# Five expert tiles instead of three started early, planned into the routing of the second batch

## What is computed

```python
x = _layernorm(x + _L0_attn_ref(...))     # causal attention, 16 heads of 16
x = _layernorm(x + _L0_ffn_ref(...))      # a linear map through an FFT, folded into one 256x256 matrix
x = _layernorm(x + _L1_attn_ref(...))     # attention over channels, one 256x256 matrix for each sequence
x = _layernorm(x + _L1_ffn_ref(...))      # 8 experts, one for each token
# the last block, on 4096 tokens:
aff = x @ centroids.T;  eid = argmax(aff);  alpha = sigmoid(sum(x * centroids[eid]))
xln = layernorm(x) * ln_g[eid] + ln_b[eid]
h = relu(xln @ w1[eid] + b1[eid])         # 256 -> 1024
out = x + alpha * (h @ w2[eid] + b2[eid]) # 1024 -> 256
```

## Time and profile before

| | us |
|---|---|
| median of 3 runs | 1402.43 (1398.66 to 1403.42) |
| the profiled execution, its own time | 1398.64 |
| its span, first to last instruction | 1396.9 |
| PE busy | 1334.6 (96%) |
| DVE busy | 1069.4 (77%) |
| ACT busy | 837.4 (60%) |
| POOL busy | 263.7 (19%) |

### The profile page before, as it was taken

The page is one execution under the profiler, slowest core; times in us unless marked ns, Lnnn a source line. Parts: engine busy times, 40 slices in busy tenths (PEclk is TensorE's granted clock), DMA queues, the critical chain, the costliest instruction groups (busy, mean ns, idle before and its releaser), DMA issues. The chain is left out here.

```text
span 1396.9 us, 45529 instructions
## 1 busy us (share of the span) xinstructions
PE 1334.6 (96%) x19106; PEld 805.1 (58%) x19106; DVE 1069.4 (77%) x1991; ACT 837.4 (60%) x1767; POOL 263.7 (19%) x440
## 2 busy tenths in 40 slices
PE   8999999999999999999999999899987799999998
PEld 3544334444444444444444444588765689999997
DVE  2567989989899899899898991566577666766766
ACT  3446668688788687787886886433455333333342
POOL 4332112102111121021021210100135411111111
PEclk9999999999999999999999999999999899999999
DMA  7796401212212212122310000314524665445441
GB/s 227 228 209 136 74 13 40 43 32 52 46 34 48 47 30 51 34 46 41 81 36 4 3 3 2 119 36 157 192 84 149 207 224 180 168 173 186 169 171 75
DMA packets 78230, 134.44 MB, mean 96 GB/s; under 512 B 12370, under 2 KB 64843, under 8 KB 72652
## 3 DMA queue, kind: packets, MB, share of 16 engines
q1 hardware_dynamic: 60556, 109.63, 26.9%
q10 hardware_dynamic: 14064, 13.47, 3.1%
q0 software_dynamic: 3408, 8.43, 1.8%
HBM read 68.01 MB, written 23.11 MB: 65 GB/s over the span
## 5 line engine op out<-in xcount | busy, mean ns | idle before, releaser
L1964 DVE TENSOR_REDUCE part_max<-pair 128x2 f32<-128x1024 f32 (+2 forms) x576 | 641.9, 1158 | 63.9 <-PE pair L1329 32.5
L1748 ACT ACTIVATE big<-pair 128x512 f32<-128x512 f32 (+1 forms) x1120 | 580.2, 607 | 151.6 <-PE pair L1360 143.5
L1360 PE MATMUL pair<-big 128*32 128x512 bf16 (+3 forms) x5120 | 347.5, 350 | 6.1 <-DMA big<-max_t 2.4
L1329 PE MATMUL pair<-big 128*32 128x512 bf16 (+3 forms) x5120 | 342.6, 349 | 9.3 <-DVE part_max L1964 8.4
L1382 PE MATMUL pair<-big 128*17 128x512 f32 (+3 forms) x2560 | 288.2, 529 | 0.9 <-POOL big L2447 0.8
L1329 PEld LDWEIGHTS pair<-big 128*32 128x32 bf16 x5120 | 130.2, 97 | 184.2 <-DVE part_max L1964 92.6
L1360 PEld LDWEIGHTS pair<-big 128*32 128x32 bf16 x5120 | 127.2, 96 | 188.7 <-ACT big L1748 117.5
L1761 ACT ACTIVATE std<-moments,eps_col 128x1 f32<-128x1 f32 (+1 forms) x102 | 30.1, 295 | 241.0 <-DVE moments L2007 240.9
L1635 PE MATMUL pair<-big,tok 128*128 128x128 f32 x1248 | 150.2, 280 | 6.5 <-DVE big L2323 6.4
L1635 PEld LDWEIGHTS pair<-big,tok 128*128 128x128 f32 x1248 | 148.5, 196 | 10.9 <-DVE big L2323 9.2
L2447 POOL TENSOR_SCALAR_AFFINE_SELECT big<-big 128x512 f32<-128x512 f32 x128 | 80.3, 637 | 323.7 <-ACT big L1748 323.7
(11 more groups left out here) (213 smaller groups left out, 1211.4 us busy)
## 6 DMA issues: line engine op xcount, KB each, us to landing
tok<-big SPq DMA_DIRECT2D x39, 1024.0 KB, 4.7
big<-in_L_ffn_w SPq DMA_DIRECT2D x16, 1024.0 KB, 14.1
big<-split_dram SPq DMA_DIRECT2D x216, 64.0 KB, 3.0
split_dram<-big ACTq DMA_DIRECT2D x32, 384.0 KB, 4.2
big<-split_dram SPq DMA_DIRECT2D x42, 256.0 KB, 4.3
big<-routed_dram SPq DMA_DIRECT2D x39, 129.0 KB, 2.1
big<-in_c_query_rows SPq DMA_DIRECT2D x8, 512.0 KB, 5.4
big<-in_L_attn_x SPq DMA_DIRECT2D x8, 512.0 KB, 4.2
```

Source lines behind the costliest of these rows:

```text
L1329: mm = pe.matmul(bank[q:q + STRIPE, o:o + w], m.q_op[slot][:, step.qt, h, step.r * P + q:step.r * P + q + STRIPE], m.k_op[slot][:, h, step ...
L1360: mm = pe.matmul(m.bank[step.bank][k:k + STRIPE, n * w:(n + 1) * w], m.k_op[slot][:, h, step.kb * P + k:step.kb * P + k + STRIPE], m.q_op[ ...
L1748: act.activation(m.p_ring[:, step.place, step.heads[0]:step.heads[-1] + 1, step.at:step.at + w], m.bank[step.bank][:, 0:len(step.heads) * ...
L1964: dve.tensor_reduce(m.part_max[(step.u * QT + step.qt) % 2][:, step.r, step.heads[0]:step.heads[0] + n, step.c], banks[:, :, 0:w], X, ALU. ...
```

## The change

1. `SOON` goes from 3 to 5. Their counts now come with route 3 (`PlaceRows` copies `count_all` after route `TPB - 1`), so `ChooseSoon` may run before any tile of batch 1 is routed.
2. The order of tiles is `C4 A2 C5 A3 C6 C7 A4 ... A7`: routes 2 and 3 come before C6 and C7.
3. The five tiles are steps of `BackPlan` (turn, four quarter hides, two half unhides on PE; rows, scale, result, final on DVE; both halves of the rectification on ACT; the sending on POOL), as are the gates, the pads and both tables. On PE a piece of an early tile has the highest rank number (5) and a handicap of 0.3 us. The dummy matmuls are gone.
4. The hides of early tiles use banks 2, 3, 4, 7 and so wait for the last C scale (`added`). Early turns share banks 0 and 1 with the A turns.
5. After the plan, each engine goes on with tile 5: PE `turn(5), hide(5), turn(6), hide(6), turn(7), unhide(5), ...`, DVE `normalise(5), turn_own(5), normalise(6), turn_own(6), rectify(5), ...`.
6. The experts' buffers have places of their own, where the eight w1 lay. `fetch_w1` reads from the input in memory, all 39 times; the loading of all eight w1 ahead is gone.
7. SP's order: `fetch_w1(0)`, five values of `tile_row`, waits for scatters 0 and 1, five row fetches, w1 of tiles 1 to 4, four pads, w1 of tile 5, rows 5 to 7, then as before.

```diff
-SOON = 3
+SOON = 5
-AFFINITY_BANKS, COUNT_BANKS, ALL_BANK = (5, 5, 5, 5, 6, 5, 6, 5), (5, 5, 5, 5, 7, 7, 7, 7), 5
+ROUTE_BANKS, SOON_BANKS = (5, 5, 5, 5, 6, 5, 6, 5), (2, 3, 4, 7)
+SOON_ORDER = [(0, "low"), (0, "high"), (1, "low"), (1, "high"), (0, "result")]
+SOON_ORDER += [piece for i in range(2, SOON) for piece in ((i, "low"), (i, "high"), (i - 1, "result"))]
+SOON_ORDER += [(SOON - 1, "result")]
-    " C0 C1 C2 C3 A0 A1 C4 C5 C6 C7 A2 A3 A4 A5 A6 A7").split()]
+    " C0 C1 C2 C3 A0 A1 C4 A2 C5 A3 C6 C7 A4 A5 A6 A7").split()]
-    SQUARES, SCALE, COMBINE = 2500, 2050, 1300
+    SQUARES, SCALE, COMBINE, SOON_LATE = 1900, 2050, 1300, 300
...
-        if engine == "pe" and added is not None and added < self.now["pe"] and idle > 600:
-            self.pe.append(Busy(int((idle - 400) / 220)))
...
-        ready = self.at(("place", TPB))
+        ready = self.at(("place", TPB - 1))
...
+    def soon_rows(self, i):
+        ready = self.at(("soon",), ("scatter", TPB - 1))
+        return None if ready is None else ready + 3000 + 600 * i
...
+            i = self.next_soon("soon turned")
+            if i < SOON:
+                ready = self.at(("soon xn", i), ("copies", len(self.turns) - 1),
+                                *([("soon xln", i - 1)] if i else []), *([("soon hidden", i - 2)] if i > 1 else []))
+                if ready is not None:
+                    yield ready, 0, self.soon_turn, (i, ready)
+            if self.soon_piece < 2 * len(SOON_ORDER):
+                q, part = divmod(self.soon_piece, 2)
+                i, what = SOON_ORDER[q]
+                ready, weights = self.soon_free(q) if part == 0 else 0, self.soon_weights(i)
+                if ready is not None and weights is not None:
+                    ready = max(ready, weights) if what == "low" else ready
+                    yield ready + self.SOON_LATE, 5, self.soon_product, (q, part, ready)
...
-        self.w1 = carve(0, [EXPERTS, KC, FF])
+        self.w1_now = [carve(i * KC * FF * 4, [KC, FF]) for i in range(W1_AHEAD)]
...
     def hide_own(i):
+        if i == SOON:
+            pe.wait_ge(s.rect_high, SOON)
+        elif i == SOON + 1:
+            pe.wait_ge(s.gated, SOON)
...
-    keep_busy(pe, m, 4)
-    turn(0)
...
-    turn(4)
+    turn(SOON)
+    hide_own(SOON)
+    turn(SOON + 1)
...
-        sp.dma_start(m.w1_now[k][:, :, :].rearrange("p c f -> p (c f)"),
-                     m.w1[:, bass.ds(e, 1), :, :].rearrange("p a c f -> p (a c f)")).then_inc(s.w1_in[k], 16)
+        sp.dma_start(m.w1_now[k][:, :, :],
+                     w1_view[bass.ds(e, 1)].rearrange("a p c f -> p (a c) f")).then_inc(s.w1_in[k], 16)
...
     sp.wait_ge(s.soon_set, 1)
-    sp.wait_ge(s.experts_in, 16 * 2 * EXPERTS)
-    sp.wait_ge(s.scatter[0], 16 * SCATTERS)
     fetch_w1(0)
     begin = [first_row(i) for i in range(SOON)]
+    sp.wait_ge(s.scatter[0], 16 * SCATTERS)
     sp.wait_ge(s.scatter[1], 16 * SCATTERS)
-    sp.wait_ge(s.product, 2 * plan.n_multiply)
     for i in range(SOON):
         fetch(i, begin[i])
-    fetch_w1(1)
+    for i in range(1, SOON):
+        fetch_w1(i)
```

More of the change, by code:

```diff
@@ L657, in turn @@
         self.todo.remove((stage, g))
-        self.run("pe", Turn(n, stage, g, before), self.TURN, ready, ("turn", n))
+        self.run("pe", Turn(n, stage, g, before, self.next_soon("soon turned")), self.TURN, ready, ("turn", n))
     def affinity_free(self, g):
[L662 to L666, removed]
+        used = last_with(ROUTE_BANKS, g)
+        return self.at(*([("hot", used), ("place", used)] if used is not None else []),
+                       *([("bias", BATCHES - 1)] if ROUTE_BANKS[g] in FOLD_BANKS else []))
     def use_choices(self):
@@ new lines, in soon_norm_choices @@
+    def soon_norm_choices(self):
+        n = self.n_norm
+        last = self.at(("end of", n - NORMS)) if n >= NORMS else 0
+        if last is None:
+            return
+        i, rows = self.next_soon("soon rows"), self.soon_rows(self.next_soon("soon rows"))
+        if i < SOON and rows is not None and (i < 2 or ("soon xn", i - 2) in self.done):
+            yield max(rows, last), 1, self.soon_moments, ("rows", i, max(rows, last))
+        i = self.next_soon("soon result")
+        if i < SOON:
+            ready = self.at(("soon unhidden", i), "soon gates")
+            if ready is not None and (i < 2 or ("soon final", i - 2) in self.done):
+                yield max(ready, last), 1, self.soon_moments, ("result", i, max(ready, last))
@@ L961, in back_plan @@
         pass
-    assert not plan.todo and plan.fold is None
+    assert not plan.todo and plan.fold is None and plan.next_soon("soon final") == SOON and "rows" in plan.done
     return plan
@@ L1676, in tensor_experts @@
             turn(i + 2)
-        unhide(i)
+        for part in range(2):
+            unhide_part(pe, m, s, i, experts[i], part)
 def scalar_loads(nc, m, s):
@@ L1853, in expert_norms @@
 def expert_norms(plan):
[L1855 to L1859 removed]
+    order = [("rows", i) for i in range(SOON, SOON + 3)]
@@ new lines, in expert_norms, with exp_gates, rectify_half @@
+    order += [what for i in range(SOON, SLOT_TILES) for what in (("rows", i + 3), ("result", i)) if what[1] < SLOT_TILES]
+    return {what: plan.n_norm + n for n, what in enumerate(order)}
+def exp_gates(act, m, s, tiles):
+    for i in tiles:
+        k = i % ROWS_AHEAD
+        act.wait_ge(s.rows_in[k], 16 * (i // ROWS_AHEAD + 1))
+        act.activation(m.gate[:, k:k + 1], m.xs[k][:, D:D + 1], ACTF.Exp, scale=-1.0).then_inc(s.gate_exp, 1)
+def rectify_half(act, m, s, i, e, half, signal):
+    col = m.columns[:, 2 * N_G:2 * N_G + N_F].rearrange("p (e c) -> p c e", c=FC)
+    act.wait_ge(s.hidden, 2 * i + half + 1)
+    for j in range(FC // 2):
+        f = half * FC // 2 + j
+        done = act.activation(m.hidden_t[i % 2][:, f, :], m.bank[hidden_bank(i, half)][:, j * P:(j + 1) * P], ACTF.Relu,
+                              bias=col[:, f, bass.ds(e, 1)])
+    done.then_inc(signal, 1)
@@ L2399, in vector_experts @@
             normalise(i + 3)
-        finish(i)
+        take_result(dve, m, s, i, experts[i], number["result", i])
+        write_final(dve, m, s, i, number["result", i])
         if (i - SOON) % 3 == 2:
-            gates([j for j in range(i + 1, i + 4) if j < SLOT_TILES])
+            set_gates(dve, m, s, [j for j in range(i + 1, i + 4) if j < SLOT_TILES])
 def pool_front(nc, m, s, plan):
```

584 lines of the change are left out of this document (333 added, 251 removed).

## The result

The changed kernel takes **1394.3 us** (median of 7 runs, 1392.21 to 1394.71). The ratio to the kernel before is 0.9947, 95% interval 0.9933 to 0.996, that is about 7.4 us faster, 5.6 to 9.4. The forecast was 1392.4, a gain of 10.0. One execution of before at 1736.11 is left out of the comparison; the six others, from 1398.66 to 1403.78, have the median 1401.3.

A forecast was written before the change was run, and what follows sets the result against it. PE, busy 96% of the span, was taken as the bound. Hide(5) at 1128.8 + 2.0 low clock + 1.8 wait + 254.3 behind it gave a span of 1386.9; 10.0 off the median made 1392.4 us, range 1385 to 1398.

The forecast's parts named there:

- T5: Start of hide(5) on PE, from which the end was written: predicted at 1128.8 us, against 1139.1 before.
- First hide, 1078: PE's first early-tile hide was to start at 1078 us, against 1099.06 before; past 1085 would mean being wrong.
- Route 3, behind C5, near 1057: Step before the first hide: at 5 to 6 us a route, route 3 was placed near 1057 us.
- Rows, not banks, set the start: Step before the first hide: fetched rows would allow it at 1077.4 us, the banks already at 1072 to 1074.
- Routing 4 us, stalls 5 us: PE between first hide and handover: 4 us of remaining routing and 5 of stalls (bounds 0 and 15) beside five tiles' 36.2.
- Pieces behind the last count: Sign of being wrong: pieces of early tiles standing behind the routing's last count.
- Handover, a new wait of 5.6 us: PE idle 5.6 us before hide(5), waiting for DVE's normalisation; then 2.0 of low clock and 1.8 before hide(6).
- w1 from memory, 0: Fetching each tile's w1 from memory instead of copying within SBUF would cost 0, hidden by 14 us.
- Last scatter by 1103: Sign on POOL: last scatter issued by 1103 us, with 25 us of room up to 1128.4.
- Table loads: ACT's two table loads of 1.28 us, as many as before; the skill's drain would add at most 2.8 us.
- Lost in the order: Rival, 19%: optimistic row time holds DVE, roots and pads hold rectifications; stalls of 11 to 19 us, about 1401 us.
- Slower: Rival, 11%: tile 5 late behind one DVE chain, with tile 4 ending after 1133 us; 1406.6 with hide(5) at 1143.

The follow-up runs named there:

- e5: Changed kernel with the last C scale and combine ahead of the early tiles' moments on DVE, affinity and A5 copies ahead of roots on ACT: 1390.71 us, ratio 0.9937.
- e7: Changed kernel with 40 unused products of 256 columns ahead of tile 5's turn and 8 ahead of its hide: 1392.0 us, ratio 0.994.
- e4: Kernel before with only each tile's w1 fetched from memory, the eight loads ahead still made but unused: 1396.5 us, ratio 0.9965.
- e10: Kernel of e4 without the loading of the eight w1 ahead: 1398.27 us, ratio 0.9978.
- e11: Kernel of e4 measured once more, unedited: 1399.01 us, ratio 0.9986.
- e2: Changed kernel with routes 2 and 3 behind C7 again, the old order of tiles: 1402.1 us, ratio 1.001.
- e3: Changed kernel with SOON = 3, three early tiles instead of five: 1399.54 us, ratio 0.9993.

## Why the prediction was right, and where it was not

The mechanism was right, and the gain smaller than forecast: 7.4 us by the ratio, 10.0 predicted. That the time came within 1.9 us of 1392.4 is in part luck. In the spans it is 1386.9 predicted and 1392.6 measured, 5.7 apart: 2.4 (C4 late, chance) + 5.9 (T5, late in the path) - 3.2 (behind T5) + 0.6 (tail 5.8 instead of 5.2). Without C4's chance 3.3 us of the gain are missing. I had then added 3.8 us, as the profiled execution of before lay that much under its median; that of the changed kernel lay 0.2 above its own, and so these 4.0 us hid most of the 5.7. Within the 3.3, two errors offset each other: T5 late by 5.9, and 3.2 won behind it.

- **First hide, 1078.** It was 1088.42, 8.1 late by the distance from C4, past the 1085 at which I called myself wrong. All times in this item have C4's 2.4 taken off where they are set against the forecast. Two steps failed.
  - "Route 3, behind C5, near 1057": place 3 ended at 1066.63, that is 1064.3, 7.3 late. I had 5 to 6 us for a route; places 1, 2 and 3 came 9.4 us apart, as did C4's, C5's and C6's multiplications, since the order has one route in each C turn. POOL was in a beta addition until 1067.93 and had the four scatters out at 1073.76, 4.4 late (1067 predicted). From there to the fetch it was 3.7 us (3.5 predicted), and from fetch to statistics it was 2.2 us instead of 3.8. So the first rows' statistics, predicted at 1074.3, came at 1079.62, 3.0 late.
  - "Rows, not banks, set the start": from the statistics to the first hide I had 3.1 us; it took 8.8. In e5 it takes 5.8 (1084.51 - 1078.75), so 3.0 of the 5.7 too much go with the order of four steps; as its rows come 0.4 us later, its first hide gains 2.7. I had seen that the planner expects the rows too early and that DVE stands at that wait, but priced it as a shift of route steps that have room, not as a wait in front of the C scale and of ACT's affinity copy. In the rows of e5 the other 2.7 us are left: the early turn stands behind an affinity turn, Best(4) stands ahead of the scale of tile 0, and 1.23 us of "issue" (where the code loads the expert's number) weren't in my chain. What each of these is worth wasn't tried.
- **Routing 4 us, stalls 5 us.** PE's five tiles went from 1088.42 to 1131.47: 43.05 us, 6.9 more than the tiles' 36.2. I had 9. PE was busy for all but 0.15 us of them:

```profile
1088.42:1131.47 43.05, 42.90 (x318) 39.32 (x317) 29.66 (x126) 20.73 (x63) 18.79 (x20) 0.94 0.54 168
```

  At a mean granted clock of 0.94 some 2.6 us, as an estimate, are the low clock behind the idle time at the start (the first two quarter hides take 1.91 and 2.06 us, later ones 1.06; the granted clock was 0.50, the lower level, from 1080 to 1090). The other 4 are the routing's pieces, as predicted. So there were next to no stalls, and together 2.2 us came back: T5 is late by 8.1 - 2.2 = 5.9.
- **Pieces behind the last count.** I had called this a sign of being wrong. It came true: the last count ran at 1111.79, and 19.5 of the five tiles' 36.2 us stand behind it. It cost nothing by itself, since PE was full on both sides of it. The sign was ill chosen: the forecast's own end of tile 4, 1123.2, lies 20 us behind its last scatter.
- **Handover, a new wait of 5.6 us.** Right: 3.83 + 0.69 + 1.11 = 5.63, ended by DVE's normalisation. Hide(5) 5.87 instead of 3.73, 2.1 against 2.0 predicted, and e7 shows that it is the clock. The bubble before hide(6) was 1.09, not 1.8.
- **w1 from memory, 0.** The landing was hidden, as argued; the value was not 0. I had asked what the load costs and not what the copy had cost others. The 2.8 us of small stalls that I carried over from before are gone in the changed kernel, as in e4, e10 and e11. They make most of the 3.2 us won behind T5.
- **Last scatter by 1103.** It was over at 1117.22 + 0.96, 15 us past that bound, since route 4's first waits for DVE until 1092.03:

```profile
1092.03 0.98 POOL L2655 DMA_INDIRECT routed_dram<-tok,position  x1 [15.50 <-DVE position L2387]
...
1117.22 0.96 POOL L2655 DMA_INDIRECT routed_dram<-tok,position  x1 [0.30 <-issue]
```

  The room for it was 25 us, up to 1128.4, and 10 of them were left: an early estimate that was wrong by 15 us decided nothing.
- **Table loads.** Behind the pads, where I had looked, ACT had for 4.84 us done nothing that the profile counts as busy, so that row couldn't tell. At 1084.51 the load begins right behind the copy before it (1084.22 + 0.27 = 1084.49), and the next instruction stands at 1085.80, 0.01 us behind its end. The drain of 1.38 us that the Trainium skill (ScalarE: Activation LUTs, What ACT_TABLE_LOAD costs) adds isn't seen here:

```profile
1084.22 0.27 ACT L1951 ACTIVATE masks<-pair 128x128 f32<-128x128 f32 x1
1084.51 1.28 ACT L2038 ACT_TABLE_LOAD   x1
```

- **The rivals.** "Lost in the order" had the right place (the optimistic row time), but the cost stood ahead of the first hide and not as stalls among the hides. "Slower" needed tile 4's end after 1133; it was 1131.47, or 1129.1 without C4's chance, nearer than the forecast's 1123.2 made it look.

The gain over before is made of routes moved up, worth 9 us (e2), which five tiles are needed to use (e3, 6 us), and stalls of 2.8 us behind hide(5) that went with the copies (e4, e10, e11). These don't simply add to 7.2: each is measured with the rest of the change in place or with none of it, and the handover's loss is new.

## What to carry to other kernels

In an order made by a greedy planner, a step that waits for a DMA is priced by what stands behind it on its engine: put the steps that need nothing from it ahead, and place it by the measured arrival. Where a change joins a planned part to a plain loop, look at the seam: the first turn and scale of the loop can stand inside the last planned tile. When a transfer is taken away, ask not only whether its replacement is hidden but what the old one slowed.

## What the runs showed of the hardware

- While 1 MB copies within on-chip memory ran, DVE waited longer, for nothing that the profile shows, ahead of the instruction that uses an expert's number: 25.5 us in 28 tiles, 1.5 at most, against 9.1 us in 13, 0.7 at most, when the same bytes came from memory, and 20.5 us in 22 when such copies were added. With its waits for PE's turn the sums are 29.3, 25.9 and 31.7 us. On ACT it was 12.8, 7.8 and 8.4 us. That it is the load of the number into a register that gets slower fits the code and isn't shown; nor is whether reading or writing on-chip memory does it.
- The unchanged first 1040 us vary by up to 4.7 us from one execution to another (C4's multiplication at 1040.00 to 1044.73). Of the 2.4 us between the two first profiles PE's waits for max_t hold 1.4 (3.8 against 2.4 us in five waits).
- Behind 3.83 and 1.11 us of idle TensorE at the handover the 32 products of hide(5) took 5.87 us, at a mean granted clock of 0.73 from 1130 to 1140; with 48 small products in the gap they took 3.81, at 1.00.
